# Sixteen small GpSimd instructions that build constants, moved from the last two batch steps to the first

## The chip, the cores and the metric

The kernel runs on one core of one Trainium2 chip. The metric is device time in microseconds (us). The engines are named as the profile names them: PE is TensorE (PEld its weight loads), DVE is VectorE, ACT is ScalarE, POOL is GpSimd, and SP is the engine that here only issues DMAs (SPq in the rows). Each engine runs its own instructions in order; engines wait for each other through semaphores.

## What is computed

One layer on x of shape (8, 256, 256) in float32: a linear-attention block and a mixture of eight experts of which each token takes two, plus a shared expert, each behind a layer norm.

```python
def attn(x):                       # x is layer-normed
    q, k, v = x @ Wq.T + bq, x @ Wk.T + bk, x @ Wv.T + bv
    phi_q, phi_k = elu(q) + 1.0, elu(k) + 1.0
    kv_sum = cumsum(phi_k * v, axis=1)
    return (phi_q * kv_sum) * SCALE @ Wo.T + bo

def ffn(x):                        # x is layer-normed, T = 2048 tokens
    logits = x @ router_w
    top_logits, top_indices = top_k(logits, 2)
    scores = softmax(top_logits)
    # each token goes through its two experts: silu(g) * u, then w2[e]
    combined = sum of the two outputs, weighted with scores
    shared = silu(x @ w_gate) * (x @ w_up) @ w_down
    return combined + shared

x = x + attn(layernorm(x))
x = x + ffn(layernorm(x))
```

## The kernel before

All matmuls are made of three float16 products (high x high, low x high, high x low), so nearly every tensor exists as a high part, which ACT writes, and a low part, which DVE writes as a difference.

The first part (to about 190 us of the trace) goes over the eight batches i = 0 to 7 as a pipeline that is written out by hand, engine by engine. A batch is 256 tokens, two tiles of 128. For each batch: layer norm 1, the projections k, v, q (`project`, L239), the attention, layer norm 2, the router's logits (`route`), the two best experts of each token, the slot of each token in its expert's list (`ranks` on PE, `slots` on DVE), and the shared expert (`gate_up`, `down`). Rows of the tokens are scattered to a table in DRAM, `x_rows`, by four indirect DMAs that POOL issues (`to_rows`, L575). The second part (from about 190 us) works through 36 blocks of 128 such rows: gather, expert up (L1100), expert down (L1125), scatter with add to the output.

What POOL does for a batch, in its own order:

- `norm1(i)` (L488 to L501) and `pow2(i)` (L513 and L515): the reciprocal square roots of the two layer norms. `pow2(i)` waits for DVE's variances (`mv`, L1511). From batch 4 on `norm2(i)` does the whole of the second one. For batches 0 to 3 DVE goes on from `pow2(i)` with `newton2(i, k)` (L1517 to L1531), four instructions, in its own order behind a wait for `pow2`.
- `gaps(i)` (L539): the difference of the two best logits, which ACT needs for the scores (`choice(i)`).
- `add_taken(i)` (L562): how many tokens each expert has so far. PE's `ranks(i + 1)` waits for it.
- `token_ids(i)` (L554): an iota into the rows of batch i. It waits until the rows of batch i - 2 have been scattered.
- `add_bo(i)` (L547): a DMA that adds the output bias to x.
- `to_rows(i)` (L575): waits for DVE's `slot_u` (L1653), the low rows (L1540) and ACT's score, then issues four indirect DMAs.

`slot_constants(k)`, for k = 0 to 3, is 8, 11, 4 and 12 small POOL instructions (35 = `N_CONST`). They make tables that depend on nothing but sizes, and count up the semaphore `slot_const`. Parts 0 and 1 stand early in POOL's order. Part 2 (L612 to L615) stands before `gaps(6)`, part 3 (L617 to L628) after `gaps(7)`, ahead of `to_rows(7)`. Inside the parts some instructions wait for the one before, by `slot_const`. The readers are DVE's plan of the blocks, PE's `spread_plan` and POOL's own work after the plan, and all of them wait for `slot_const` to be 35; the plan begins on DVE at L1869, at 175.7 us of the trace.

After `pow2(2)` and `newton2(2, k)` the way goes on as follows: ACT's `normed2(2)` (L1238) makes the normed rows, `row_hi2(2)` (L1247) their high part, and behind them in ACT's order stands `silu(4)` (L1254), for which PE's `gate_up(1, 1)` (L239, `bG`) waits; DVE's `row_lo(1, 2)` (L1540) makes the low part, and SP then turns the rows with two DMA transposes (`turn2`, L378), for which PE's `route` waits. `turn1` (L368) is the same for layer norm 1.

Of the kernel before, what the change touches and what calls it, by code (L numbers as in the profile page):

```python
# [32 lines left out]
def layer_kernel(nc, x, w_att, w_bias, w_bo, w_shared, w_expert, out):  # L33
# [33 lines left out]
    with ExitStack() as ctx:  # L67
# [394 lines left out]
        def _(pool):  # L462
# [20 lines left out]
            def norm1(i):  # L483

                at = PLN * (i - 2)
                pool.wait_ge(S["mv1_done"], TB * (i - 1))
                pool.wait_ge(S["xn1"], TB * i)
                pool.tensor_scalar(ve[0][:], mv[0][:, :, 1], EPS, None, ALU.add).then_inc(S["pln"], 1)  # L488
                pool.wait_ge(S["pln"], at + 1)
                pool.tensor_tensor(y0[0][:], ve[0][:], minus_half[:], ALU.pow).then_inc(S["pln"], 1)  # L490
                pool.wait_ge(S["pln"], at + 2)
                pool.tensor_tensor(nt_[0][:], y0[0][:], y0[0][:], ALU.mult).then_inc(S["pln"], 1)
                pool.wait_ge(S["pln"], at + 3)
                pool.tensor_tensor(nu[0][:], nt_[0][:], ve[0][:], ALU.mult).then_inc(S["pln"], 1)
                pool.wait_ge(S["pln"], at + 4)
                pool.tensor_scalar(nw[:], nu[0][:], 0.5, -1.5, ALU.mult, ALU.add).then_inc(S["pln"], 1)
                pool.wait_ge(S["pln"], at + 5)
                pool.tensor_tensor(neg[:], nw[:], y0[0][:], ALU.mult).then_inc(S["pln"], 1)
                pool.wait_ge(S["pln"], at + 6)
                pool.tensor_tensor(shift[0][:], mv[0][:, :, 0], neg[:], ALU.mult).then_inc(S["pln"], 1)  # L500
                pool.tensor_scalar(rstd[0][:], neg[:], -1.0, None, ALU.mult).then_inc(S["norm1_done"], 1)  # L501
# [15 lines left out]
            def norm2(i):  # L517

                at = 4 * (i - ON_DVE)
                pow2(i)  # L520
                pool.wait_ge(S["pow2"], i + 1)
                pool.tensor_tensor(nt_[1][:], y0[1][:], y0[1][:], ALU.mult).then_inc(S["pln2"], 1)
                pool.wait_ge(S["pln2"], at + 1)
                pool.tensor_tensor(nu[1][:], nt_[1][:], ve[1][:], ALU.mult).then_inc(S["pln2"], 1)
                pool.wait_ge(S["pln2"], at + 2)
                pool.tensor_scalar(nw2[:], nu[1][:], 0.5, -1.5, ALU.mult, ALU.add).then_inc(S["pln2"], 1)
                pool.wait_ge(S["pln2"], at + 3)
                pool.tensor_tensor(neg2[:], nw2[:], y0[1][:], ALU.mult).then_inc(S["pln2"], 1)
                pool.wait_ge(S["pln2"], at + 4)
                pool.wait_ge(S["xn2"], TB * i)  # L530
                pool.tensor_scalar(rstd[1][:], neg2[:], -1.0, None, ALU.mult).then_inc(S["norm2_done"], 1)
                pool.tensor_tensor(shift[1][:], mv[1][:, :, 0], neg2[:], ALU.mult).then_inc(S["norm2_done"], 1)

            def gaps(i):

                pool.wait_ge(S["top_done"], TB * (i + 1))
                if i >= 1:
                    pool.wait_ge(S["tanh_done"], i)
                pool.tensor_tensor(dlog[:], top[:, :, 0], top[:, :, 1], ALU.subtract).then_inc(S["dlog_done"], 1)  # L539

            def add_bo(i):

                pool.wait_ge(S["xn1"], TB * (i + 1))
                if i >= 2:
                    pool.wait_ge(S["x1_done"], i - 1)
                pool.nop(nofuse=True)
                pool.dma_start(xs_of(i), bo[:].rearrange("p (o d) -> p o d", o=1).to_broadcast((P, TB, D)),  # L547
                               accum_op=ALU.add).then_inc(S[f"xbo{i % 2}"], 16)

            def token_ids(i):  # L550

                if i >= 2:
                    pool.wait_ge(*saved_before(i))
                pool.iota(row_tok[i % 2], pattern=[[P, TB], [1, 1]], base=i * L, channel_multiplier=1).then_inc(S["tok_done"], 1)  # L554

            def add_taken(i):

                pool.wait_ge(S["taken_done"], i + 1)
                pool.wait_ge(S["oh_done"], i + 1)
                if i >= 1:  # L560
                    pool.wait_ge(S["rank_ps"], i)
                pool.tensor_tensor(taken[(i + 1) % 2][:], taken[i % 2][:], oh[i % 2][:], ALU.add).then_inc(S["taken_done"], 1)  # L562

            def to_rows(i):

                q = i % 2
                pool.wait_ge(S["l2_done"], i + 1)
                pool.wait_ge(S["tok_done"], i + 1)
                pool.wait_ge(S["t_done"], i + 1)
                pool.wait_ge(S["topi_done"], TB * (i + 1))  # L570
                pool.wait_ge(S["slot_done"], i + 1)
                pool.nop(nofuse=True)
                for t in range(TB):
                    for k in range(2):
                        pool.indirect_dma_start(xrows, bass.IndirectOffsetOnAxis(ap=slot_u[q][:, k, t:t + 1], axis=0),  # L575
                                                rows2[q][:, t, :].bitcast(U16), None).then_inc(S[f"saved{q}"], 16)
# [76 lines left out]
            pow2(1)  # L653
            norm1(3)
            gaps(0)
            add_taken(0)
            to_rows(0)
            add_bo(3)
            gaps(1)
# [11 lines left out]
            for i in range(4, B):  # L671
                if i < B - 1:
                    norm1(i + 1)
                else:
                    slot_constants(2)
                gaps(i - 1)
                if i < B - 1:
                    add_bo(i + 1)
                token_ids(i)
                norm2(i)  # L680
                add_taken(i - 1)
                to_rows(i - 1)
            gaps(B - 1)
            slot_constants(3)
            to_rows(B - 1)


# [777 lines left out]
        def _(dve):  # L1465
# [189 lines left out]
            def expert_lo(p):  # L1655
                dve.wait_ge(S["ex_hi"], p + 1)
                (hi, src), (lo, _) = expert_part(p, 0), expert_part(p, 1)
                dve.scalar_tensor_tensor(out=lo, in0=src, scalar=WS, in1=hi, op0=ALU.mult, op1=ALU.subtract  # L1658
                                         ).then_inc(S["ex_lo"], 1)

            def shared_lo(m, h):
                dve.wait_ge(S["sh_hi"], SHARED.index((m, h)) + 1)
                (hi, src), (lo, _) = shared_part(m, h, ws_h), shared_part(m, h, ws_l)
                dve.scalar_tensor_tensor(out=lo, in0=src, scalar=WS, in1=hi, op0=ALU.mult, op1=ALU.subtract
                                         ).then_inc(S["sh_lo"], 1)
# [352 lines left out]
```

## Time and profile before

| | us |
|---|---|
| median of 3 runs | 353.23 |
| lowest, highest | 353.05, 353.76 |
| the profiled execution, its time | 353.23 |
| the profiled execution, its span | 351.3 |

The span is the time from the first to the last instruction in the trace; 1.93 us of the execution's time lie around it. The profiled execution took exactly the median, so differences that are worked out on its span can be added to the median. The granted TensorE clock is 0.999 of full speed over the span. A row of a timeline gives the start of an instruction or a run of equal ones, its duration, engine, line and operands, and in brackets how long the engine had been idle before it and what ended that.

### The profile page before, as it was taken

Reading aid. Unit: us, or ns where it says so; the run is one execution under the profiler, and the core shown is the slowest. Engines: PE = TensorE matmul, PEld = TensorE weight load, DVE = VectorE, ACT = ScalarE, POOL = GpSimd, SP = SyncE. Lnnn points to the kernel's source line nnn. Section 1 sums busy time; section 2 is a strip of 40 time slices with the busy share of each in tenths; the row PEclk is TensorE's granted clock in tenths of the full one; section 3 lists DMA queues with packets and bytes.
Section 4 is the critical chain, followed back from the end, with each engine's and each line's share of the span. In section 5 each row is a group of like instructions: output and inputs, shape, how many; then the busy total and the mean of one; then the engine's idle time right before and its main releaser. Section 6 shows DMA issues by size and latency. Waiting matters only on the chain.

```text
span 351.3 us, 9142 instructions
## 1 busy us (share of the span) xinstructions
PE 339.7 (97%) x2926; PEld 256.5 (73%) x2926; DVE 235.4 (67%) x585; ACT 213.8 (61%) x389; POOL 192.7 (55%) x282
## 2 busy tenths in 40 slices
PE   7999989999999999999999999999999999999993
PEld 7779878888888898888988465656656566666662
DVE  4999989899799887978788464453544533334441
ACT  2678949787887987746536444455544445544551
POOL 4777567785866768565357443353433445443335
PEclk9999999999999999999999999999999999999999
DMA  6992151556875556735775348658585866966740
GB/s 191 386 350 50 21 136 43 131 149 166 196 200 91 150 166 141 213 112 131 250 257 122 93 66 114 88 89 100 73 118 78 100 101 84 108 99 93 91 72 10
DMA packets 76108, 45.90 MB, mean 131 GB/s; under 512 B 59936, under 2 KB 71200, under 8 KB 75680
## 3 DMA queue, kind: packets, MB, share of 16 engines
q1 hardware_dynamic: 62000, 34.82, 40.4%
q0 software_dynamic: 9392, 10.44, 19.0%
q10 hardware_dynamic: 4672, 0.07, 1.1%
q8 instruction: 26, 0.43, 0.5%
q14 instruction: 18, 0.15, 0.2%
HBM read 19.09 MB, written 12.97 MB: 91 GB/s over the span
## 4 chain that ended last, share of the span: by engine, by line
PE 80%; DVE 8%; DMA 5%; issue 2%; ACT 2%; SPq 1%; POOL 1%; POOLq 0%; DVEq 0%; ACTq 0%
PE bU L1100 13%; PE bG L1100 13%; PE bD L977 8%; PE bU L239 7%; PE bG L239 7%; PE bQ L1125 6%; PE bV L1125 6%; PE bV L239 3%; PE bK L239 3%; DMA xT<-rows 2%; PE bK L1080 2%; PE bQ L239 2%; PE bT L977 2%; DMA wd<-in_w_att 1%; DVE ab L1602 1%
## 5 line engine op out<-in xcount | busy, mean ns | idle before, releaser
L1602 DVE SCALAR_TENSOR_TENSOR ab<-bU,sg 128x512 f32<-128x512 f32 x64 | 44.1, 689 | 66.2 <-PE bU L1100 50.8
L778 POOL DMA_INDIRECT out_y<-xs,dst_row x32 | 50.0, 1564 | 61.0 <-DMA out_y<-xs,dst_row 27.8
L1254 ACT ACTIVATE sg<-bG 128x512 f32<-128x512 f32 x64 | 38.0, 593 | 44.5 <-PE bG L1100 25.9
L1100 PE MATMUL bG<-we,work 128*128 (+1 forms) x216 | 52.6, 380 | 0.0
L1100 PE MATMUL bU<-we,work 128*128 (+1 forms) x216 | 52.6, 379 | 0.0
L575 POOL DMA_INDIRECT x_rows<-rows,slot_u x32 | 40.6, 1270 | 19.0 <-issue 14.5
L1419 ACT ACTIVATE ws_h<-ab 128x512 f16<-128x512 f32 x36 | 22.7, 629 | 41.5 <-DVE ab L1602 38.9
L1924 DVE TENSOR_TENSOR ws_h<-ab,ws_h 128x512 f16<-128x512 f32 x36 | 25.0, 693 | 20.8 <-ACT ws_h L1419 20.2
L1261 ACT ACTIVATE ah<-ab 128x512 f16<-128x512 f32 x32 | 20.1, 628 | 28.0 <-DVE ab L1602 23.8
L1100 PEld LDWEIGHTS bG<-we,work 128*128 128x128 f16 (+1 forms) x216 | 20.7, 99 | 19.3 <-issue 1.6
L1100 PEld LDWEIGHTS bU<-we,work 128*128 128x128 f16 (+1 forms) x216 | 19.8, 99 | 17.4
L1125 PE MATMUL bV<-wd,ws_l 128*128 (+1 forms) x216 | 27.0, 273 | 0.0
L1125 PE MATMUL bQ<-wd,ws_l 128*128 (+1 forms) x216 | 26.8, 273 | 0.0
L1125 PEld LDWEIGHTS bV<-wd,ws_l 128*128 128x128 f16 (+1 forms) x216 | 21.1, 99 | 6.8 <-issue 1.9
L1125 PEld LDWEIGHTS bQ<-wd,ws_l 128*128 128x128 f16 (+1 forms) x216 | 21.0, 99 | 6.9 <-issue 1.7
L773 POOL DMA_INDIRECT out_y<-xs,half_dst x8 | 12.3, 1542 | 22.5 <-issue 9.2
L239 PE MATMUL bU<-xT,ws_h 128*128 128x256 f16 x144 | 24.6, 273 | 0.0
L239 PE MATMUL bG<-xT,ws_h 128*128 128x256 f16 x144 | 24.5, 273 | 0.0
L1607 DVE TENSOR_TENSOR al<-ab,ah 128x512 f16<-128x512 f32 x32 | 21.7, 678 | 1.9 <-ACT ah L1261 1.8
L1426 ACT ACTIVATE ws_l<-bK 128x512 f16<-128x512 f32 x36 | 21.3, 592 | 0.6 <-PE bK L1080 0.6
L1658 DVE SCALAR_TENSOR_TENSOR we<-stage,we 128x1024 f16<-128x1024 f32 x16 | 19.6, 1223 | 0.8 <-ACT we L1281 0.5
L1080 PEld LDWEIGHTS bK<-ident,ws_h 128*128 128x128 f16 x144 | 10.6, 98 | 9.9 <-issue 1.6
(337 smaller groups left out, 815.2 us busy)
## 6 DMA issues: line engine op xcount, KB each, us to landing
stage<-in_w_expert SPq DMA_DIRECT2D x24, 512.0 KB
we<-in_w_shared SPq DMA_DIRECT2D x3, 1024.0 KB, 11.9
out_y<-xs SPq DMA_DIRECT2D x8, 256.0 KB
xs<-bo POOLq DMA_DIRECT2D x7, 256.0 KB, 4.4
xs<-in_x SPq DMA_DIRECT2D x1, 1280.0 KB, 17.2
x_rows<-we SPq DMA_DIRECT2D x9, 134.0 KB
xs<-in_x SPq DMA_DIRECT2D x3, 256.0 KB, 4.0
work<-x_rows SPq DMA_TRANSPOSE x40
```

The source lines that it names most:

```text
L239: ins = pe.matmul(dst, a(c), b(c), start=s == 0 and c == 0, stop=s == 2 and c == n - 1)
L575: pool.indirect_dma_start(xrows, bass.IndirectOffsetOnAxis(ap=slot_u[q][:, k, t:t + 1], axis=0), rows2[q][:, t, :].bitcast(U16), None).the ...
L778: pool.indirect_dma_start(out_rows, bass.IndirectOffsetOnAxis(ap=dst_row[:, b:b + 1], axis=0), ya[b % NY], None, bounds_check=NT * P - 1, ...
L977: ins = pe.matmul(dst[:, t * D:(t + 1) * D], a[:, at:at + P], w[:, 2 * f + c, :], start=f + s + t + c == 0, stop=f == NP - 1 and s == 2 an ...
L1100: ins = pe.matmul(dst[t * n:(t + 1) * n, :], x2[:, hi * KC + k, t * n:(t + 1) * n], w[t][lo][:, k, half, :], start=s == 0 and k == 0, stop ...
L1125: ins = pe.matmul(dst[t * m:(t + 1) * m, :], a[:, c, t * m:(t + 1) * m], w[t][:, c, lo, :], start=s == 0 and c == 0, stop=s == 2 and c == ...
L1254: act.activation(sg[q][:], src[:], ACT.Silu, scale=1.0 / WS).then_inc(S["sg_done"], 1)
L1419: act.activation(ar_h[n], ab[b % 2][:], ACT.Copy).then_inc(S["ah_done"], 1)
L1426: act.activation(aT_h[n].rearrange("p c l -> p (c l)"), bK[:], ACT.Copy).then_inc(S["ath_done"], 1)
L1602: dve.scalar_tensor_tensor(out=ab[q][:], in0=src[:], scalar=1.0 / WS, in1=sg[q][:], op0=ALU.mult, op1=ALU.mult).then_inc(S["a_done"], 1)
L1607: dve.tensor_tensor(al[f][:], ab[f % 2][:], ah[f][:], ALU.subtract).then_inc(S["al_done"], 1)
L1924: dve.tensor_tensor(ar_l[n], ab[b % 2][:], ar_h[n], ALU.subtract).then_inc(S["al_done"], 1)
```

## The change

Part 2 of the constants now stands on POOL right behind `gaps(0)`, and part 3 right behind `add_taken(0)`, ahead of `to_rows(0)`. Both leave their former places. No instruction is added or taken away, and the order on PE, DVE, ACT and SP is the same.

```diff
@@ -653,7 +653,9 @@
             norm1(3)
             gaps(0)
+            slot_constants(2)
             add_taken(0)
+            slot_constants(3)
             to_rows(0)
             add_bo(3)
             gaps(1)
@@ -671,8 +673,6 @@
             for i in range(4, B):
                 if i < B - 1:
                     norm1(i + 1)
-                else:
-                    slot_constants(2)
                 gaps(i - 1)
                 if i < B - 1:
                     add_bo(i + 1)
@@ -681,7 +681,6 @@
                 add_taken(i - 1)
                 to_rows(i - 1)
             gaps(B - 1)
-            slot_constants(3)
             to_rows(B - 1)
```

On POOL, at the first batch's routing (`dlog` is `gaps(0)`, `taken` is `add_taken(0)`, the DMA of four is `to_rows(0)`, the second `dlog` is `gaps(1)`, `ve` and `y` are `pow2(2)`), before the change:

```order
L539 TENSOR_TENSOR dlog<-top 128x2
L562 TENSOR_TENSOR taken<-taken,oh 128x32
L575 DMA x_rows<-rows,slot_u 17536x536 x4
L547 DMA xs<-bo 128x2x256
L539 TENSOR_TENSOR dlog<-top 128x2
L513 TENSOR_SCALAR ve<-mv 128x2
L515 TENSOR_TENSOR y<-ve,minus_half 128x2
```

And at the same place with the change:

```order
72 L539 TENSOR_TENSOR dlog<-top 128x2
73 L612 TENSOR_SCALAR slot_w<-mix_at,slot_w 128x4
74 L613 TENSOR_SCALAR mix_past<-mix_at,slot_w 128x4
75 L614 TENSOR_TENSOR slot_w<-slot_w,upper 128x1
76 L615 TENSOR_SCALAR pick_block<-iota_f,slot_w 128x36
77 L562 TENSOR_TENSOR taken<-taken,oh 128x32
78 L617 TENSOR_TENSOR mix_thr<-mix_thr,slot_w 128x4
79 L618 TENSOR_TENSOR mix_row<-mix_row,slot_w 128x4
80 L619 TENSOR_TENSOR at_slot<-slot_w 128x2
81 L620 TENSOR_TENSOR slot_w<-mix_thr,mix_past 128x4
82 L621 TENSOR_TENSOR slot_w<-mix_row,mix_past 128x4
83 L622 TENSOR_TENSOR at_slot<-at_slot 128x1
```

Six more of part 3 (L623 to L628) follow, and then the four indirect DMAs, `add_bo(3)`, `gaps(1)` and `pow2(2)` in the order of before: four instructions have come between `gaps(0)` and `add_taken(0)`, and twelve between `add_taken(0)` and `to_rows(0)`.

On POOL, at the last batch's routing (`dlog` is `gaps(7)`, the DMA is `to_rows(7)`), before the change, with the first and the last row of part 3:

```order
176 L539 TENSOR_TENSOR dlog<-top 128x2
177 L617 TENSOR_TENSOR mix_thr<-mix_thr,slot_w 128x4
178 L618 TENSOR_TENSOR mix_row<-mix_row,slot_w 128x4
...
187 L627 TENSOR_SCALAR spread_w<-ones,at_slot 128x64
188 L628 TENSOR_SCALAR spread_w<-ones,at_slot 128x64
189 L575 DMA x_rows<-rows,slot_u 17536x536 x4
```

And with the change, from `to_rows(6)` on:

```order
187 L575 DMA x_rows<-rows,slot_u 17536x536 x4
188 L539 TENSOR_TENSOR dlog<-top 128x2
189 L575 DMA x_rows<-rows,slot_u 17536x536 x4
190 L700 TENSOR_SCALAR tok_at<-row_at,ends_at 128x1 x2
191 L707 DMA tok_id<-x_rows,tok_at 128x1 x2
```

Here the twelve have gone from between `gaps(7)` and `to_rows(7)`; likewise the four of part 2 have gone from ahead of `gaps(6)`.

## Rows read from the trace of the kernel before

**Rows 1.** The page: busy time of each engine; chain that ended last, by engine.

```profile
PE 339.7 (97%) x2926; PEld 256.5 (73%) x2926; DVE 235.4 (67%) x585; ACT 213.8 (61%) x389; POOL 192.7 (55%) x282
...
PE 80%; DVE 8%; DMA 5%; issue 2%; ACT 2%; SPq 1%; POOL 1%; POOLq 0%; DVEq 0%; ACTq 0%
```

**Rows 2.** The chain in order of time: start us, us, what.

```profile
42.47 3.12 DMA xT<-rows
...
55.31 1.09 ACT xn L1238 x2
...
77.05 5.65 DMA xT<-rows
```

**Rows 3.** Waits of PE, 0 to 200 us: total us, times, longest us.

```profile
PE bR L239 <- DMA xT<-rows: 1.4, 2, 0.9
```

**Rows 4.** Timeline of POOL, 142 to 176 us: parts 2 and 3 at their old places.

```profile
142.15 0.32 POOL L612 TENSOR_SCALAR slot_w<-mix_at,slot_w 128x4 f32<-128x4 f32 x1
...
144.25 0.89 POOL L615 TENSOR_SCALAR pick_block<-iota_f,slot_w 128x36 f16<-128x36 f32 x1
148.79 0.19 POOL L539 TENSOR_TENSOR dlog<-top 128x2 f32<-128x2 f32 x1 [3.65 <-issue]
...
168.02 0.20 POOL L617 TENSOR_TENSOR mix_thr<-mix_thr,slot_w 128x4 f32<-128x4 f32 x1
...
170.67 0.45 POOL L628 TENSOR_SCALAR spread_w<-ones,at_slot 128x64 f16<-128x64 f16 x1
175.61 1.13 POOL L575 DMA_INDIRECT x_rows<-rows,slot_u  x1 [4.49 <-DVE slot_u L1653]
```

**Rows 5.** Timeline of POOL, 37 to 54 us: the new place.

```profile
37.39 0.19 POOL L539 TENSOR_TENSOR dlog<-top 128x2 f32<-128x2 f32 x1
37.55 1.25 POOL L562 TENSOR_TENSOR taken<-taken,oh 128x32 f16<-128x32 f16 x1
42.46 1.17 POOL L575 DMA_INDIRECT x_rows<-rows,slot_u  x1 [3.66 <-issue]
...
46.98 1.41 POOL L575 DMA_INDIRECT x_rows<-rows,slot_u  x1 [0.30 <-issue]
48.39 1.36 POOL L547 DMA_DIRECT2D xs<-bo  x1
49.24 0.74 POOL L539 TENSOR_TENSOR dlog<-top 128x2 f32<-128x2 f32 x1
53.00 0.56 POOL L513 TENSOR_SCALAR ve<-mv 128x2 f32<-128x2 f32 x1 [3.02 <-DVE mv L1511]
53.65 0.73 POOL L515 TENSOR_TENSOR y<-ve,minus_half 128x2 f32<-128x2 f32 x1
```

**Rows 6.** Timeline of DVE, 37 to 55 us, beside the new place.

```profile
37.48 2.40 DVE L1664 SCALAR_TENSOR_TENSOR ws_l<-we,ws_h 128x1024 f16<-128x1024 f32 x2
...
44.02 1.22 DVE L1664 SCALAR_TENSOR_TENSOR ws_l<-we,ws_h 128x1024 f16<-128x1024 f32 x1
...
45.76 1.22 DVE L1565 TENSOR_TENSOR_SCAN work<-keep,work 128x512 f32<-128x512 f16 x1
...
54.41 0.16 DVE L1517 SCALAR_TENSOR_TENSOR nt<-y 128x2 f32<-128x2 f32 x1
```

**Rows 7.** Timelines of POOL and of DVE at 24.9 us: an instruction of part 1.

```profile
24.95 1.08 POOL L600 TENSOR_TENSOR at_slot<-at_slot,upper 128x1 f32<-128x1 f32 x1
...
24.84 1.22 DVE L1565 TENSOR_TENSOR_SCAN work<-keep,work 128x512 f32<-128x512 f16 x1
```

**Rows 8.** DVE's scan L1565 over the span: duration ns least, median, most; starts.

```profile
L1565 DVE TENSOR_TENSOR_SCAN work<-keep,work x8: 1211/1224/1396, 16.3 to 142.2; 128x512 f32<-128x512 f16 x8
```

**Rows 9.** Timeline of ACT: `silu(4)`, behind `normed2(2)` and `row_hi2(2)`.

```profile
56.95 0.58 ACT L1254 ACTIVATE sg<-bG 128x512 f32<-128x512 f32 x1
```

**Rows 10.** Timeline of PE: `gate_up(1, 1)` and `route(3)`.

```profile
57.59 0.39 PE L239 MATMUL bG<-xT,ws_h 128*128 128x256 f16 x2
...
82.75 0.26 PE L239 MATMUL bR<-wa_h,xT 128*128 128x8 f16 x4 [0.55 <-DMA xT<-rows]
```

## The prediction

> **What bounds the kernel now.** I read the page first: PE is busy for 339.7 of 351.3 us and holds 80% of the chain that ended last, POOL is busy 55% of the span and holds 1% of the chain [rows 1]. So POOL's work costs nothing in itself. It costs where someone on PE's path waits for POOL, and there each engine's timeline has to be read around the two places of the change. Next I read PE's waits: between 0 and 200 us the largest is for the transposed rows, twice, 1.4 us together [rows 3]; one of the two is `route(3)`, which starts at 82.75 after 0.55 us of waiting [rows 10], so the other is 0.9 us. Behind 82.75 PE has no wait in the batch part that is over 0.2 us, so whatever PE is late there it is late to the end. Then I read the chain in order of time: at 55.31 it goes through ACT's `normed2(2)`, and at 77.05 through a transposing DMA that takes 5.65 us [rows 2]. Around 55 us it is therefore not PE but the second layer norm of batch 2 that decides.
>
> **What the change takes away.** The four instructions of part 2 run from 142.15 to 145.14 (144.25 + 0.89), 3.0 us, and behind them POOL is idle for 3.65 us until `gaps(6)` at 148.79. The twelve of part 3 run from 168.02 to 171.12, 3.1 us, and behind them POOL is idle for 4.49 us until DVE's `slot_u` lets `to_rows(7)` go at 175.61 [rows 4]. In both places the wait for DVE swallows what is removed: `gaps(6)` and `to_rows(7)` start when they started before. The readers of the constants begin at 175.7, 4.6 us behind the end of part 3, so they gain nothing either. One thing may be gained: DVE's scan took 1396 ns at its longest, against a median of 1224 ns [rows 8], and the last of the eight starts at 142.2 and is that one, beside the first instruction of part 2. That is 0.17 us of DVE, off PE's path there. The removal is worth 0, at most 0.2 us.
>
> **What it adds, on POOL.** In the new place POOL has a gap: `add_taken(0)` ends at 38.80 and `to_rows(0)` starts at 42.46, 3.66 us later, since it waits for DVE's slots [rows 5]. Sixteen instructions have to fit between 37.58, the end of `gaps(0)`, and 42.46 less the 0.5 us that an unhindered `to_rows` needs to get going.
>
> How long they take depends on DVE. A small POOL instruction takes 0.2 us when nothing hinders it (`gaps(0)`, 0.19), but `add_taken(0)` takes 1.25 us, from 37.55 to 38.80 [rows 5], and ends 0.1 us behind the first of the two 1.2 us instructions L1664 that DVE started at 37.48 [rows 6]. An instruction of part 1, as small, takes 1.08 us beside DVE's scan, which started 0.11 before it and ended 0.03 after it [rows 7]. All these DVE instructions read two operands from SBUF. So I take it that a POOL instruction that reads SBUF ends when such a DVE instruction does, and that about one POOL instruction gets through between two of them. The Trainium skill, "SBUF — State Buffer", section "Who interferes with whom", states the same as a rule: a DVE instruction with two SBUF inputs and a GpSimd instruction that reads SBUF contend, and the second to issue waits for the first to finish. These two rows agree with it.
>
> From 37.48 to 46.98 DVE runs nine such instructions, nearly without a gap: L1664 twice, L1607, two low rows (L1540, L1537), L1551, L1664 again at 44.02, L1607, and the scan at 45.76 [rows 6], which show the first two, the seventh and the ninth. Laying the sixteen beside them: L612 ends with the first L1664 at 38.8, L613 with the second at 40.0, L614 with L1607 at 40.6, L615 (wider) at 41.3. `add_taken(0)`, L617 and L618 fit in the free 0.8 us up to 41.9; L619 and L620 come through by 42.7, L621 behind L1551 at 43.3; L622 to L625 run free to 44.0; L626 ends behind the L1664 of 44.02 at 45.3, L627 behind L1607 at 46.1 and L628 behind the scan at 47.2. With luck at two of the handovers the end is 46.1, without it 47.8. The bound from below is the rate at the old place, 3.1 us for twelve [rows 4], hence 4.1 for sixteen: the end at 41.9, which would be hidden in the gap altogether. I take 47.2, since it follows DVE's own order there; the old place of part 3 has DVE working on other things.
>
> Then `to_rows(0)` starts near 47.7 instead of 42.46. Its four DMAs took from 42.46 to 48.39, 5.9 us, of which some 0.8 was also waiting beside the DVE instructions up to 48.3; behind that DVE has none before 52.8. So they take 5.3, and `add_bo(3)` starts at 53.0 instead of 48.39. From its start to the end of `gaps(1)` was 1.6 us (49.98 less 48.39) [rows 5], so `pow2(2)` can start at 54.6. It started at 53.00, and had waited 3.02 us for DVE's variances. So 3.0 of the 4.6 us are covered, and it starts 1.6 late. It has no DVE instruction beside it this time (DVE stands waiting for it): 0.25 + 0.08 + 0.73 us, and `y` is there at 55.6 instead of 54.38. With the early end (46.1) it is there at 54.5, with the late one (47.8) at 55.7.
>
> **What it adds, on the path.** DVE's `newton2(2, 0)` starts at 54.41, right behind `pow2(2)` (53.65 + 0.73) [rows 5, 6]: no slack. Behind it on DVE wait `slots(1)`, the keys of batch 3 and the low rows of batch 2. Its four instructions take 0.8 us, then ACT's `normed2(2)` follows, which started at 55.31 [rows 2], 0.1 us behind DVE's end: a slack of 0.1. On ACT, `row_hi2(2)` and `silu(4)` stand behind it; `silu(4)` ends at 57.53 [rows 9], and PE's `gate_up(1, 1)`, which waits for it, starts at 57.59 with no idle time of PE's own [rows 10]: a slack of 0. So PE is late by 55.6 - 54.4 - 0.1 = 1.1 us with the middle value, 0.0 with the early, 1.2 with the late one. Since every handover that comes out differently here takes off rather than adds (one place to slip in saves about 0.6), I carry 0.85 on.
>
> Behind that everything hangs on the same shifted DVE: the low rows of batch 3 and SP's two transposes for `route(3)` come 0.85 later, as PE does. But PE waited 0.55 us there, since one transfer took 5.65 us where the like one took 3.12 [rows 2, 10]. If it is slow again, PE keeps the whole 0.85. If it takes 3.1 it ends at 81.0, 2 us before PE asks for it, the 0.55 are gone, and PE is 0.3 late. POOL's later steps, `norm1(4)` and `to_rows(1)`, move with DVE and ACT and add nothing.
>
> What may come back early: PE waited 0.9 us at `route(1)` [rows 3] for the transposes of batch 1, which ran beside the first of `to_rows(0)`'s scatters; with these later the transposes may be faster. But the next matmuls, `project(3)`, wait for two further transposes that SP issues only behind those, and the 57.59 is set by POOL in any case. I count 0.
>
> **The sum.** 0.3 to 0.85 on the path, and nothing back: between the two I take 0.65, so 353.23 + 0.65 = 353.9. The profiled execution is itself the median, with 351.3 of span and 1.93 around it; its span would be 352.0. A difference of 0.2% is 0.7 us, about what a measurement of this kernel can tell from no change; the forecast stands at the edge of it.
>
> **The rivals.**
> - The gap hides it. If POOL's sixteen run at the rate of the old place, or DVE's instructions let two pass at a time, they end by 44.6 or so and `pow2(2)` starts at 53.00 as before: 353.2. Against it stand the 1.25 and 1.08 us. For it: 3.0 us of cover at `pow2(2)` come on top of the 3.66.
> - Faster. The delay on POOL is hidden (end up to 46.1), and the later scatter leaves the transposes free: the 0.55 us at `route(3)` go and 0.2 more. 353.23 - 0.75 = 352.5. It decides if `pow2(2)` ends before 54.5 and the transfer of batch 3 takes under 5.0 us.
> - More than that: the handover also goes the other way. The scan that took 0.17 us too long [rows 8] shows a POOL instruction ahead of a DVE one and DVE waiting. Fifteen of the sixteen read SBUF; if half of them cost DVE 0.1 each ahead of SP's issue, transposes for `route(1)` come up to 0.4 late, and `token_ids(2)`, which waits for the scatter of batch 0 (its last DMA now issued at 53.0), may hold up `norm1(4)`, `to_rows(1)` and so `pow2(3)` as well, for some 0.4: 353.23 + 1.1 + 0.4 = 354.7. By the skill's rule too, order of issue alone decides who waits, so it allows both directions; it puts no figure on the share.
> - The change does not do what it says: the constants could be read before they are made or the scatter wait for them. Every reader waits for all 35, far later; I give it nothing.
>
> **How the numbers follow.** Late by 0.3 to 0.85, forecast: 0.54. Hidden, 353.2: 0.18. Faster, 352.5: 0.12. More, 354.7: 0.16. Of the forecast's 0.54 about half lies over the 0.7 us, so slower has 0.16 + 0.26 = 0.42, same 0.18 + 0.28 = 0.46, faster 0.12. The range from 352.8 to 354.9 leaves out most of the fast case and the far end of the slow one.
>
> **What would show it.** On POOL, the fifteen reading instructions at 37.5 to 47 should show several of 0.6 to 1.2 us, and `to_rows(0)` should start near 47.7 with no idle wait for DVE. `pow2(2)` should have no idle time before it, and DVE's L1517 some in front, released by POOL. PE should wait at `gate_up(1, 1)` for ACT. The gaps ahead of `gaps(6)` and `to_rows(7)` should grow by 3.0 and 3.1 us. It is wrong if `pow2(2)` still starts on DVE's `mv`, or if PE's start at `gate_up(1, 1)` is late and the end is not.

## The result, and the profile after

The changed kernel takes 356.29 us (median of 5, 355.04 to 356.74), the one before 353.23 (median of 5, 352.88 to 353.76): a ratio of 1.0077 with a 95% interval of 1.0053 to 1.0100. It is slower, and by more than the range allowed (352.8 to 354.9). The profiled execution took 355.62 us, 2.39 more than that of before, and its span is 353.8, 2.5 more. From line 685 of the kernel before on, line numbers of the changed kernel are lower by one: L1253 is `silu`, L1516 the first line of `newton2` in DVE.

The page, in the same two lines as [rows 1]:

```profile
PE 340.5 (96%) x2926; PEld 257.2 (73%) x2926; DVE 234.9 (66%) x585; ACT 214.1 (61%) x389; POOL 194.9 (55%) x282
...
PE 74%; DVE 10%; POOL 7%; DMA 4%; issue 3%; SPq 1%; ACT 1%; POOLq 0%; DVEq 0%; ACTq 0%
```

Busy times hardly differ (POOL has 2.2 us more, for the same 282 instructions), but POOL's share of the chain that ended last went from 1% to 7%. The timeline of POOL, 37 to 57 us, shows why; it answers to [rows 5]. Its first line is taken from DVE's timeline (a pair of 1.2 us instructions):

```profile
37.37 2.35 DVE L1663 SCALAR_TENSOR_TENSOR ws_l<-we,ws_h 128x1024 f16<-128x1024 f32 x2
...
37.28 0.20 POOL L539 TENSOR_TENSOR dlog<-top 128x2 f32<-128x2 f32 x1
37.45 2.36 POOL L612 TENSOR_SCALAR slot_w<-mix_at,slot_w 128x4 f32<-128x4 f32 x1
39.80 1.22 POOL L613 TENSOR_SCALAR mix_past<-mix_at,slot_w 128x4 f32<-128x4 f32 x1
...
43.93 1.24 POOL L623 TENSOR_TENSOR at_slot<-at_slot 128x1 f32<-128x1 f32 x1
...
47.75 0.74 POOL L628 TENSOR_SCALAR spread_w<-ones,at_slot 128x64 f16<-128x64 f16 x1
48.67 1.17 POOL L575 DMA_INDIRECT x_rows<-rows,slot_u  x1 [0.18 <-issue]
...
54.05 1.37 POOL L547 DMA_DIRECT2D xs<-bo  x1
...
55.74 0.23 POOL L513 TENSOR_SCALAR ve<-mv 128x2 f32<-128x2 f32 x1
56.05 0.72 POOL L515 TENSOR_TENSOR y<-ve,minus_half 128x2 f32<-128x2 f32 x1
```

The sixteen end at 48.49 (47.75 + 0.74). `to_rows(0)` starts 6.2 us later than before (48.67 against 42.46), and `pow2(2)` has lost its wait for DVE's variances and starts 2.74 us late. Its `y` is there at 56.77 instead of 54.38. The chain goes on through DVE and ACT to PE; these are rows of their three timelines, which answer to [rows 6, 9, 10]:

```profile
56.81 0.16 DVE L1516 SCALAR_TENSOR_TENSOR nt<-y 128x2 f32<-128x2 f32 x1 [2.59 <-POOL y L515]
57.60 1.09 ACT L1237 ACTIVATE xn<-xs,shift,rstd 128x256 f32<-128x256 f32 x2 [2.47 <-DVE shift L1530]
59.26 0.58 ACT L1253 ACTIVATE sg<-bG 128x512 f32<-128x512 f32 x1
59.89 0.39 PE L239 MATMUL bG<-xT,ws_h 128*128 128x256 f16 x2 [2.44 <-ACT sg L1253]
```

Each engine waits for the one ahead, with the same 2.4 to 2.6 us. PE's waits between 0 and 200 us, in the view of [rows 3], now begin so:

```profile
PE bG L239 <- ACT sg L1253: 2.4, 1, 2.4
...
PE bK L239 <- DMA xT<-rows: 1.0, 2, 0.9
```

PE starts `gate_up(1, 1)` at 59.89, 2.30 us late. It then waits a second time, at `route(2)`, where it had no wait before:

```profile
64.46 0.26 PE L239 MATMUL bR<-wa_h,we 128*128 128x8 f16 x4 [0.45 <-DMA we<-rows]
```

This wait hangs on the same `y`, by the other way: DVE's low part of the rows, then SP's two transposes, which start at 60.10 instead of 57.83. The chain that ended last runs this way, from `pow2(2)` over DVE, SP and the DMA to `route(2)`, and not over `silu(4)`. At `route(2)` PE is 2.66 us late (64.46 against 61.80), and at the end of the span still 2.5.

At the two old places nothing was gained. Here is POOL's timeline there, to be read against [rows 4]:

```profile
151.29 0.19 POOL L539 TENSOR_TENSOR dlog<-top 128x2 f32<-128x2 f32 x1 [6.64 <-DVE top L1622]
...
178.08 1.03 POOL L575 DMA_INDIRECT x_rows<-rows,slot_u  x1 [7.46 <-DVE slot_u L1652]
```

The wait ahead of `gaps(6)` grew from 3.65 to 6.64 us and that ahead of `to_rows(7)` from 4.49 to 7.46: 3.0 us each, and both steps start 2.5 late, as the whole batch part does.

### The profile page after: what moved, and what is told of

It is laid out like the page before. It is cut to its first block, busy times and chain, and to the rows that moved or that the text cites. A ratio compares the mean times of both kernels' runs of the same rounds, so it can differ in the third digit from the quotient of the medians.

```text
span 353.8 us, 9142 instructions
## 1 busy us (share of the span) xinstructions
PE 340.5 (96%) x2926; PEld 257.2 (73%) x2926; DVE 234.9 (66%) x585; ACT 214.1 (61%) x389; POOL 194.9 (55%) x282
## 4 chain that ended last, share of the span: by engine, by line
PE 74%; DVE 10%; POOL 7%; DMA 4%; issue 3%; SPq 1%; ACT 1%; POOLq 0%; DVEq 0%; ACTq 0%
PE bU L1099 13%; PE bG L1099 13%; PE bD L976 8%; PE bG L239 7%; PE bU L239 7%; PE bQ L1124 6%; PE bV L1124 6%; PE bV L239 3%; PE bK L239 3%; PE bK L1079 2%; PE bT L846 2%; DMA xT<-rows 1%; PE bT L976 1%; DVE st L1468 1%; POOL x_rows L575 1%
## 5 line engine op out<-in xcount | busy, mean ns | idle before, releaser
L1253 ACT ACTIVATE sg<-bG 128x512 f32<-128x512 f32 x64 | 38.0, 593 | 44.9 <-PE bG L1099 26.4
L1923 DVE TENSOR_TENSOR ws_h<-ab,ws_h 128x512 f16<-128x512 f32 x36 | 24.9, 693 | 20.8 <-ACT ws_h L1418 19.6
```

The lines of the kernel that those rows point to most:

```text
L1253: act.activation(sg[q][:], src[:], ACT.Silu, scale=1.0 / WS).then_inc(S["sg_done"], 1)
L1923: dve.tensor_tensor(ar_l[n], ab[b % 2][:], ar_h[n], ALU.subtract).then_inc(S["al_done"], 1)
```

## The experiments

Three questions were open. Is the late `pow2(2)` all of the loss? Why did the sixteen end at 48.5 and not at 47.2? And why is the median 0.7 us over the profiled execution? The theory was that POOL alone carries the loss, by way of `pow2(2)`. Its rivals were that the moved instructions hold up DVE, and that the later scatters disturb the transposes. Each kernel was measured together with the kernel before (medians 353.25 to 353.31), and the ratios are against that.

**Where the loss enters: `pow2(2)`.** First, part 2 alone in its new place, with part 3 back in its old one:

```diff
             gaps(0)
+            slot_constants(2)
             add_taken(0)
...
-                else:
-                    slot_constants(2)
```

> Only the four instructions of part 2 stand early; part 3 is back ahead of to_rows(7). Theory (POOL is late at pow2(2), and by as much as the constants outlast the gap ahead of to_rows(0)): L612 to L615 end near 41.4 and add_taken(0) near 41.9 as in the changed kernel, so to_rows(0) starts at 42.4 to 42.9, pow2(2) still waits for DVE: 353.2, within 0.3 of before. Rival (already the later add_taken(0), or the loss at the old place, costs): a third or more of the 3 us, 354.2 or above.

353.91 us (median of 10, 353.22 to 354.27), a ratio of 1.0013 [1.0002, 1.0025]. Its POOL timeline:

```profile
42.88 1.45 POOL L575 DMA_INDIRECT x_rows<-rows,slot_u  x1 [0.80 <-issue]
...
53.71 0.57 POOL L513 TENSOR_SCALAR ve<-mv 128x2 f32<-128x2 f32 x1 [2.90 <-DVE mv L1510]
```

`to_rows(0)` is only 0.4 us late, and `pow2(2)` keeps 2.9 us of slack: POOL costs nothing here. The median is up by 0.7 us (0.13% by the ratio, 0.5 us), more than the 0.3 expected, and this comes from elsewhere. PE's timeline shows it ahead of `pow2(2)`:

```profile
48.47 0.39 PE L239 MATMUL bK<-xT,wa_h 128*128 128x256 f16 x2 [1.63 <-DMA xT<-rows]
```

`project(3)` started at 47.75 before and is now 0.7 us late for its transposes, though SP issued them within 0.1 us of the old times. (Some 0.1 us of it was there before the moved work: `gaps(0)` starts at 37.49, not 37.39.) What changed nearby is POOL's four scatters, which start 0.4 to 1.3 us later. That they are what delays the transposes is likely but not shown: this is one trace, and which packets met which was not separated.

Next, the changed kernel with `add_bo(3)`, which POOL issues ahead of `gaps(1)`, put behind `pow2(2)`:

```diff
-            add_bo(3)
             gaps(1)
             pow2(2)
+            add_bo(3)
```

> The changed kernel with add_bo(3) behind pow2(2) instead of ahead of gaps(1). Theory: pow2(2) comes 1.4 us earlier (the duration of the add_bo issue) and everything behind it too: 1.3 to 1.5 us under the changed kernel, about 354.9. PE's wait at gate_up(1, 1) falls from 2.4 to about 1.0 us. Rival (the late scatter and its traffic cost, not pow2(2)): the scatter is as late as in the changed kernel, so 356.3, unchanged.

354.20 us (median of 7, 353.88 to 354.45), 1.0029 [1.0018, 1.0041]. In its POOL timeline `pow2(2)` comes 1.6 us earlier than in the changed kernel (`ve` 55.74 there), and PE's waits follow:

```profile
54.14 0.23 POOL L513 TENSOR_SCALAR ve<-mv 128x2 f32<-128x2 f32 x1
...
PE bG L239 <- ACT sg L1253: 1.1, 1, 1.1
```

PE's wait fell from 2.4 to 1.1 us, and it starts `gate_up(1, 1)` at 58.29, 1.6 us earlier. The profiled executions are 1.74 us apart (355.62 and 353.88), as that would have it. The medians are 2.1 apart, more than was expected; of that more below. The scatter itself is as late as in the changed kernel (`to_rows(0)` at 48.45), and this execution takes only 0.65 us more than that of before: so a late scatter, without a late `pow2(2)`, explains little of the loss.

To have the lateness of `pow2(2)` without any of the moved work, the kernel before got seven pow instructions ahead of `pow2(2)`, which write to `extra`, a part of `dst_row` that is unused at that time:

```diff
+            extra = dst_row[:].bitcast(F32)
...
+                for n in range(lo, hi):
+                    pool.tensor_tensor(extra[:, 2 * n:2 * n + 2], ve[0][:], minus_half[:], ALU.pow)
...
             gaps(1)
+            extras(0, 7)
             pow2(2)
```

> The kernel before, constants at the old places, with seven extra power instructions (0.72 us each) between gaps(1) and pow2(2). The scatter of batch 0, add_bo(3) and add_taken(0) are on time. Theory (pow2(2) alone carries the delay): 5.0 us from 50.0, y of pow2(2) ready at 56.0 instead of 54.4, DVE idle ahead of L1517, PE waits 1.5 us at gate_up(1, 1): 354.7 to 355.0. Rival (a late scatter is needed for a loss): 353.2.

354.76 us (median of 4, 354.60 to 354.94), 1.0044 [1.0028, 1.0061]. POOL's timeline and PE's waits:

```profile
49.38 5.17 POOL L634 TENSOR_TENSOR dst_row<-ve,minus_half 128x2 f32<-128x2 f32 x7
54.63 0.24 POOL L513 TENSOR_SCALAR ve<-mv 128x2 f32<-128x2 f32 x1
...
PE bG L239 <- ACT sg L1261: 1.2, 1, 1.2
```

Everything up to 49.4 us is as it was before. `y` is late by 1.28 us (55.66 against 54.38), PE by 1.21, the time by 1.5. The path through `newton2`, `normed2` and `silu` has no slack to speak of, as the prediction had it.

The real sixteen were also put in that place, behind `gaps(1)` and ahead of `pow2(2)`:

```diff
             gaps(1)
+            slot_constants(2)
+            slot_constants(3)
             pow2(2)
```

> Both parts of the constants stand behind gaps(1), right ahead of pow2(2), instead of around add_taken(0). DVE has few two-input instructions there (49.5 to 52.8 us). Theory (the price of the sixteen is what outlasts POOL's cover, and most of their length at the changed kernel's place is waiting for DVE): they take 4 to 4.9 us from 50.0, so pow2(2) starts at 54.2 to 54.9, PE is 1.0 us late at gate_up(1, 1), 354.1 to 354.5. Rival (the length belongs to the instructions themselves, 10 us at any place): pow2(2) starts at 60, 7 us late, 360.

354.42 us (median of 7, 354.10 to 356.08), 1.0040 [1.0025, 1.0056]. The first starts at 49.19, and POOL's timeline gives the last, and `pow2(2)`:

```profile
53.67 0.45 POOL L628 TENSOR_SCALAR spread_w<-ones,at_slot 128x64 f16<-128x64 f16 x1
54.20 0.23 POOL L513 TENSOR_SCALAR ve<-mv 128x2 f32<-128x2 f32 x1
```

The same sixteen take 4.9 us where few of DVE's two-operand instructions run, against 11.0 us in the changed kernel (37.45 to 48.49, with 0.2 of `add_taken(0)` among it). PE is 0.8 us late. What they cost hangs on what DVE does beside them.

**Why the sixteen took so long.** The kernel before got sixteen small reading instructions in place of the sixteen, four ahead of `add_taken(0)` and twelve behind it; nothing else moved.

```diff
+                    pool.tensor_scalar(extra[:, 2 * n:2 * n + 2], half_f[:, 0:2], 1.0, None, ALU.mult)
...
             gaps(0)
+            extras(0, 4)
             add_taken(0)
+            extras(4, 16)
```

> The kernel before, with its constants at the old places, and sixteen extra POOL instructions at the new places (four and twelve), each reading two elements from SBUF and writing two that nobody reads. Theory (a POOL instruction that reads SBUF waits for DVE's two-input instructions): they last until 44.5 to 48, to_rows(0) starts late, +0 to +2.5 us, most likely +1.5: 354.7; several of them take 0.6 us or more. Rival (only their count matters): 16 x 0.16 = 2.6 us, ended at 40.9, nothing lost: 353.2.

352.98 us (median of 10, 352.68 to 354.27), 0.9993 [0.9982, 1.0003]: no change, where a loss had been expected.

```profile
37.62 3.55 POOL L634 TENSOR_SCALAR dst_row<-half_f 128x2 f32<-128x2 f32 x4
...
41.35 4.02 POOL L634 TENSOR_SCALAR dst_row<-half_f 128x2 f32<-128x2 f32 x12
45.53 1.38 POOL L575 DMA_INDIRECT x_rows<-rows,slot_u  x1 [0.17 <-issue]
...
52.92 0.56 POOL L513 TENSOR_SCALAR ve<-mv 128x2 f32<-128x2 f32 x1 [0.33 <-DVE mv L1519]
```

`to_rows(0)` comes 3.1 us late and `pow2(2)` still waits 0.33 for DVE. So the cover is real: by this row it reaches until `to_rows(0)` starts at about 45.9 (45.53 + 0.33). What comes later than that is lost but for 0.4 us: the changed kernel's 48.67 is 2.8 beyond it and its `y` 2.4 late, mostly since `ve` takes 0.23 us with DVE idle beside it, not 0.56. The plain reads are 3.1 us quicker than the real sixteen.

Next, sixteen memsets, which write and do not read:

```diff
+                    pool.memset(extra[:, 2 * n:2 * n + 2], 0.0)
```

> As the kernel with sixteen extra reads, but with sixteen memsets, which write as much and read nothing. Theory: none of them waits for DVE, 0.1 us each, all hidden in the gap of 3.66 us: 353.2, to_rows(0) at 42.5. Rival (any POOL instruction waits for DVE, or it is the number of instructions): as slow as the sixteen reads.

353.18 us (median of 10, 352.71 to 353.75), 0.9994 [0.9984, 1.0004].

```profile
37.48 0.19 POOL L634 MEMSET dst_row<- 128x2 f32 x4
...
38.70 0.42 POOL L634 MEMSET dst_row<- 128x2 f32 x12
42.41 1.17 POOL L575 DMA_INDIRECT x_rows<-rows,slot_u  x1 [3.29 <-issue]
```

In the same places the twelve take 0.42 us, not 4.02. It is the reading beside DVE that costs, not the instructions.

Three differences between the plain reads and the real ones were then taken one by one. First, size: three of the sixteen as wide as the real ones, 36 and twice 64 elements, the others as before.

```diff
+                    if n == 3:
+                        pool.tensor_scalar(pick_block[:], iota_f[:, 0:NBLK], 1.0, None, ALU.mult)
+                    elif n >= 14:
+                        half = slice((n - 14) * HALF, (n - 13) * HALF)
+                        pool.tensor_scalar(spread_w[:, half], ones16[:, half], 1.0, None, ALU.mult)
```

> The sixteen extra reads without waits, of which the 4th reads 36 elements and the last two read 64 each, as in parts 2 and 3. If the width makes the difference: the last two take 0.7 to 1.0 us each beside DVE and the end is at 46.5 to 47.5, +0.5 to +1.5. If not: the end is at 46.0 at the latest (0.27 us more for each of the two wide ones, 0.15 for the third), pow2(2) starts at 53.0 to 53.3, 353.2 to 353.5.

353.54 us (median of 10, 353.01 to 354.13), 1.0007 [0.9998, 1.0017].

```profile
46.13 1.72 POOL L575 DMA_INDIRECT x_rows<-rows,slot_u  x1 [0.17 <-issue]
```

`to_rows(0)` starts 0.6 us later than with narrow reads. Second, waits between them. The real ones depend on one another, so some wait on a semaphore; here a wait stands behind the 4th, 7th, 10th and 11th:

```diff
+                    pool.tensor_scalar(extra[:, 2 * n:2 * n + 2], half_f[:, 0:2], 1.0, None, ALU.mult).then_inc(S["extra"], 1)
+                    if n + 1 in (4, 7, 10, 11):
+                        pool.wait_ge(S["extra"], n_extra[0])
```

> The sixteen extra reads as before, now with a wait for the one before behind the 4th, 7th, 10th and 11th, as parts 2 and 3 have. The plain ones ended at 45.4 and cost nothing, the real ones at 48.5. If the waits make the difference (each lets DVE's next instruction in first): the end is at 47 to 48.5, to_rows(0) starts at 47.3 or later and the time is 1.5 to 2.5 above before. If the waits are only their own 0.1 us each: the end is at 45.8, pow2(2) still waits for DVE, 353.2.

354.80 us (median of 4, 353.71 to 355.68), 1.0054 [1.0036, 1.0072].

```profile
41.15 5.59 POOL L636 TENSOR_SCALAR dst_row<-half_f 128x2 f32<-128x2 f32 x12
46.92 1.42 POOL L575 DMA_INDIRECT x_rows<-rows,slot_u  x1 [0.17 <-issue]
...
PE bG L239 <- ACT sg L1266: 0.7, 1, 0.7
```

The twelve take 5.59 us instead of 4.02: behind a wait the next one starts later, and twice it started just behind a DVE instruction and lost a turn to it. (A turn is the time until one such DVE instruction ends.) `to_rows(0)` starts 1.4 us later than with plain reads, beyond the 45.9, and PE waits 0.7. The end, 46.7, is a little earlier than expected. The profiled execution is only 0.48 us over that of before, and the other three are 0.9 to 2.0 us slower than it; why, no run shows. Third, the operand: the first instruction, L612, took 2.36 us in the changed kernel, L613 half of that. Both multiply by a value from SBUF, one for each partition. The plain reads were given such a value:

```diff
-                    pool.tensor_scalar(extra[:, 2 * n:2 * n + 2], half_f[:, 0:2], 1.0, None, ALU.mult)
+                    pool.tensor_scalar(extra[:, 2 * n:2 * n + 2], half_f[:, 0:2], row_f[:], None, ALU.mult)
```

> The sixteen extra reads without waits, but each multiplies with a scalar that it reads from SBUF, as L612 and L613 do (they took 2.36 and 1.22 us where the plain reads took 1.23 and 1.16 and then 0.64). If the second operand from SBUF costs a second turn beside DVE: the first takes 2.3 us, the second 1.2, the sixteen end at 47 or later, 354.5 to 356. If not: they end at 45.4 as the plain ones, 353.0 to 353.3.

357.47 us (median of 4, 356.48 to 357.82), 1.0109 [1.0089, 1.0129]. POOL's timeline, PE's waits, and then the sixteen by line, with shortest, median and longest duration in ns, first in this kernel and then with the plain number:

```profile
37.81 4.06 POOL L634 TENSOR_SCALAR dst_row<-half_f,row_f 128x2 f32<-128x2 f32 x4
...
42.06 7.65 POOL L634 TENSOR_SCALAR dst_row<-half_f,row_f 128x2 f32<-128x2 f32 x12
49.88 1.15 POOL L575 DMA_INDIRECT x_rows<-rows,slot_u  x1 [0.17 <-issue]
...
PE bG L239 <- ACT sg L1262: 3.1, 2, 2.9
...
L634 POOL TENSOR_SCALAR dst_row<-half_f,row_f x16: 284/288/2347, 37.8 to 49.4; 128x2 f32<-128x2 f32 x16
```

```profile
L634 POOL TENSOR_SCALAR dst_row<-half_f x16: 207/216/1219, 37.6 to 44.2; 128x2 f32<-128x2 f32 x16
```

The longest is 2347 ns against 1219: the first, beside the same pair of DVE's 1.2 us instructions, loses two turns where the plain one loses one. Four of these sixteen lost two turns, of the plain ones none. Unhindered, the operand costs 0.07 us (median 288 against 216). With all sixteen so, the end moves from 45.4 to 49.7 us, and the time is above the range that was expected. In the real sequence L612, L613, L615, L627 and L628 have such a scalar. L613 lost two turns as well, though short ones: it ends at 41.02, just behind the second of two 0.68 us instructions that DVE has there. If the three effects simply add, widths give 0.6 and waits 1.4 of the 3.1 us between plain and real reads, and these operands the other 1.1. Counted from `gaps(0)` of the same execution, since the executions differ by up to 0.3 us ahead of it, they are 0.8, 1.7 and 0.8 of 3.3. The last figure is a remainder either way and was not measured by itself.

**Why the median is above the profiled execution.** The changed kernel was run again, unchanged.

> The changed kernel as it is, once more. Theory: the length of the sixteen beside DVE is the same in every execution (L612 took 2.35 or 2.36 in all three kernels that have it there), so pow2(2) starts at 55.7 again and PE waits 2.4 us at gate_up(1, 1); the spread of 1.7 us between its executions must then come from somewhere else, behind 60 us. If the handovers vary, the start of to_rows(0) is another one than 48.67.

356.50 us (median of 4, 355.87 to 357.05), 1.0096 [1.0079, 1.0113], and its profiled execution took 355.87. POOL's rows are those above to within 0.08 us (L612 2.36, `to_rows(0)` at 48.62, `ve` at 55.68), and PE waits the same 2.4 us. So the two profiled executions agree in all of POOL's part. But both are quick ones, below their medians, so this does not exclude that POOL's part differs in the slower ones. Then, both parts behind `add_taken(0)`:

```diff
             gaps(0)
-            slot_constants(2)
             add_taken(0)
+            slot_constants(2)
             slot_constants(3)
```

> The changed kernel with add_taken(0) ahead of part 2 instead of between the parts. add_taken(0) then spends the first L1664 (1.2 us) and L612 meets the second. If L612 takes two turns wherever it meets DVE: it ends at 40.5 after 1.8 us, and the sixteen end within 0.3 us of before (48.2 to 48.8), 355.5 to 356.3. If its 2.36 us come from meeting the first of two L1664: it takes 1.2 here, and everything is up to 0.6 us earlier.

356.98 us (median of 4, 356.49 to 357.99), 1.0110 [1.0087, 1.0132]. POOL's timeline:

```profile
38.56 1.79 POOL L612 TENSOR_SCALAR slot_w<-mix_at,slot_w 128x4 f32<-128x4 f32 x1
...
48.58 1.17 POOL L575 DMA_INDIRECT x_rows<-rows,slot_u  x1 [0.18 <-issue]
```

L612 starts beside the second of the DVE pair and ends at 40.35, behind two DVE instructions (the pair ends at 39.65, the next at 40.26): two turns in another place. `to_rows(0)` comes within 0.1 us of the changed kernel, and so does PE: the order of `add_taken(0)` does not matter. But the profiled execution took 356.94, above what was expected and 1.3 more than the changed kernel's. PE's timeline behind the wait shows it:

```profile
59.81 0.39 PE L239 MATMUL bG<-xT,ws_h 128*128 128x256 f16 x2 [2.44 <-ACT sg L1253]
...
60.26 1.03 PE L239 MATMUL bG<-xT,ws_h 128*128 128x256 f16 x4
...
63.65 0.41 PE L239 MATMUL bU<-xT,ws_l 128*128 128x256 f16 x2
...
64.11 0.60 PE L976 MATMUL bD<-ws_h,ah 128*128 128x256 f16 x4
```

Four matmuls take 1.03 us where they take 0.60 at 64.11. The table by stage says the same for 60 to 64 us: stretch, its length, busy time and count of PE, PEld, DVE, ACT and POOL, granted clock, DMA share, GB/s. First this kernel, then the changed one:

```profile
60.00:64.00 4.00, 4.00 (x23) 2.94 (x22) 3.51 (x5) 3.52 (x6) 2.92 (x4) 0.57 0.48 118
```

```profile
60.00:64.00 4.00, 4.00 (x36) 3.26 (x35) 4.00 (x7) 3.50 (x6) 2.93 (x4) 1.00 0.46 109
```

After a PE wait of 2.44 us the granted clock is 0.57 over these 4 us, so for most of them the lower of the two levels, 1.2 GHz, where the changed kernel's profiled execution has 1.00, 2.4 GHz, behind a wait of the same length. PE comes to the `bD` matmuls at 64.11 instead of 62.53, 1.58 later. The wait for the transposed rows at `route(2)` is gone in return, and 0.96 stay there (65.42 against 64.46), 1.13 at `route(3)` (85.96 against 84.83). The kernel with a value from SBUF shows the same behind its 2.9 us wait: 0.65 over 60 to 64 us and 0.92 over 64 to 68.

All eight profiled executions in which PE waits for `silu(4)` can be laid side by side: by how much PE is late at `gate_up(1, 1)`, and by how much the execution is slower than that of before. In the six whose clock stayed up, the second is the first to within 0.4 us (2.30 and 2.39 in the changed kernel, 2.24 and 2.64 when run again, 0.70 and 0.65 with `add_bo(3)` behind). In the two whose clock fell it is 1.5 us more: 2.22 and 3.71, 3.13 and 4.59.

This may be the rest of the median. 1.2 instead of 2.4 GHz from 60.3 to 63.7 us takes 0.005 off the granted clock of a whole execution (half of 3.4 in 355 us). Of the changed kernel's ten executions three have 0.993 or 0.994 and average 356.65 us; the seven others average 355.93. With both parts behind `add_taken(0)` three of four are that low, with `add_bo(3)` behind `pow2(2)` none is below 0.996. That is a reading of few executions, not a proof, and three things speak against leaning on it. First, 356.74 at 0.995, 356.42 at 0.997 and 356.39 at 0.998 don't fit. Second, the clock of a whole execution doesn't tell where it fell: in the profiled executions with memsets and with the constants behind `gaps(1)`, both at 0.995, it stayed up at 60 to 68 us and fell at 348 to 352 us (0.52 and 0.58), where PE has nothing left to do, and the kernel before has one at 0.994 that takes 353.71. Third, executions spread without it too: 356.08 at 0.999 with the constants behind `gaps(1)`, and the 353.71 to 355.68 of the reads with waits, at 0.996 to 0.998. So where the clock was seen to fall it costs some 1.1 to 1.5 us. How much of the changed kernel's 0.7 is from it, and what decides in which executions it falls, stays open.

## Why the prediction was wrong

**What held.** The removal is worth 0, down to the two waits that grew by 3.0 us. The path was named right up to `gate_up(1, 1)`: POOL's reads beside DVE, `to_rows(0)`, `add_bo(3)`, `pow2(2)`, `newton2`, `normed2(2)`, `silu(4)`, PE, with 3.0 us of cover at `pow2(2)` and none behind it. The other branch, by DVE and the transposes to `route(2)`, was not in it; it added 0.4 us there. The rule cited from the Trainium skill ("SBUF — State Buffer", "Who interferes with whom") agrees with the memsets, which read nothing and took 0.42 us where twelve reads took 4.02. It does not give the second turn of L612, which started at 37.45 and still let the DVE instruction of 38.50 end first. The rival by which the gap hides it was wrong for the real sixteen and right for sixteen plain reads; no run was faster, as the other had it. The rival by which DVE is held up has no support, though its 354.7 is nearest to the result: DVE's L1663 of 43.91 and scan of 45.64 come 0.11 and 0.12 us earlier than in [rows 6], and so does the pair of 37.37, ahead of them all (0.11): nothing was added between. `token_ids(2)` had no wait either.

**The step that failed: laying the sixteen beside DVE.** The prediction let each POOL instruction end with the next DVE instruction, so L612 at 38.8 and L613 at 40.0. L612 ended at 39.81 and L613 at 41.02: a turn more than assumed, in rows that have a scalar operand in SBUF. Only instructions without one had served as measure (`add_taken(0)`, an instruction of part 1). DVE's free stretch gave part of this turn back (L621 ended at 43.71, not 43.3). But L623, which was to run free, then started at 43.93, 0.02 us behind a DVE instruction of 1.2 us, and lost another. The waits between the instructions, which the prediction put at nothing, cost 1.4 us among plain reads. The end was given as 47.2, at the latest 47.8, and it was 48.49. This term was short by 1.3 us, and its late bound was no bound: it was the same walk with worse luck, so an error of the rule was not in it.

That the end was missed by no more than 1.3 us is in part luck. For sixteen plain narrow reads, to which the rule applies as it stands, it would have been 1.8 us too late (45.4 instead of 47.2), since more of them pass in DVE's free stretches than the prediction let through: five from 43.28 to 44.20 alone. The two errors partly cancel.

The steps behind it added what they should: `add_bo(3)` 54.05 against 53.0, `y` 56.77 against 55.6. (Of the 0.5 us that the prediction gave `to_rows` to get going, the trace shows 0.18.) PE was late by 2.30 us, where the prediction's own middle value was 1.1.

**The credits.** From 1.1 the prediction went down to 0.85, since "every handover that comes out differently here takes off rather than adds", and to 0.65 as the middle between keeping that and losing 0.55 us of PE's wait at `route(3)`. The first was the wrong way round. The second came about and was not kept: `route(3)` starts at 84.83, 2.08 us late instead of 2.66 at `route(2)`, but by `project(5)` at 96.31 PE is 2.57 late again, with this row in its timeline:

```profile
96.31 0.39 PE L239 MATMUL bK<-xT,wa_h 128*128 128x256 f16 x2 [0.17 <-DMA xT<-rows]
```

The transfers for `project(5)` are late with everything else behind DVE. By the same pattern the 0.9 us at `route(1)` went (PE 0.88 us earlier at 44.83) and came back as a wait of 0.87 us at `project(3)`; that one the prediction had counted as 0, and at `route(3)` it didn't follow its own reasoning. Without the credits the forecast would have been 354.3, inside its range and still 2.0 below the median.

**What was in neither the sum nor the rivals.** PE's clock, and the spread of the executions. PE is 2.30 us late at `gate_up(1, 1)` and 2.5 at the end, and the profiled execution, in which the clock stays up, is 2.39 over that of before. The median is 3.06 over. The 0.7 us between may be the half clock of some executions, which no run isolated. The 2.4 us between forecast and result are thus 1.2 from the laying, 0.45 from the credits, and 0.8 from behind `gate_up(1, 1)`, most of it open. A new wait of 2.4 us on PE can cost more than its length, and the upper end of the range should have had room for that.

None of the versions beats the kernel before. The nearest to it are plain reads and memsets, which do nothing for it, with intervals that include 1.

## What to carry to other kernels

- A gap on an engine is cover only up to the next deadline behind it. Find that deadline first (here `to_rows(0)` at about 45.9 us, 3.4 us behind its old start), and then ask what the moved work takes in its new surroundings, not in its old ones: the same sixteen instructions took 4.9 us in one place and more than twice that in another.
- Price small POOL instructions by form. Beside DVE instructions with two operands in SBUF, one that reads a tensor loses a turn, one whose scalar also comes from SBUF up to two, one behind a semaphore wait can lose the next turn too, and a memset none. So lay them by their form, and give the rule itself an error in the late bound.
- A wait that vanishes at one transfer is kept only if the next consumer of the same producer isn't late as well. Leave such credits out unless its row is shown.

## What the runs showed of the hardware that was not expected

- POOL's `tensor_scalar` with its scalar in SBUF lost two turns beside back-to-back DVE instructions of 1.2 us: 2.35 or 2.36 us in five executions of the kernels here, against 1.22 for one with a plain number. With four waits among the sixteen plain reads the last twelve took 5.59 us, without waits 4.02.
- Behind a PE wait of 2.4 to 2.9 us, ahead of which PE had been busy for all of 52 to 56 us, the granted clock fell to 1.2 GHz in two profiled executions, from 60.3 to 63.7 us in the one shown. In two others, of the changed kernel, with a wait of 2.44 us, it stayed at 2.4 GHz. Behind waits of 0.7 to 1.2 us (four kernels) it stayed there in every profiled execution.
